# A two-layer cross-attention kernel: queries laid once over two halves of the partitions

## What is computed

```python
q_hk  = (hidden_q @ Wq.T).reshape(B, S, H, K)
q_big = einsum('bshk,hkq->bshq', q_hk, w_kc_q)        # 192 wide
q_big = apply_rope(q_big, sin_q, cos_q)               # layer 0 only
kv_r  = apply_rope(kv_c, sin_k, cos_k)                # 1500 x 64
q_r   = einsum('bshq,hqr->bhsr', q_big, W_qr)
k_r   = einsum('bld,hdr->bhlr', kv_r, W_kr)
attn  = softmax(einsum('bhsr,bhlr->bhsl', q_r, k_r))
ctx_c = einsum('bhsl,bld->bhsd', attn, kv_r)
out   = einsum('bhsd,hkd->bshk', ctx_c, w_kc_kv).reshape(B, S, H*K) @ Wo.T
```

## Time and profile before

| | |
|---|---|
| median of 3 runs | 3490.61 us (3485.57 to 3497.17) |
| profiled execution: its time | 3502.88 us |
| profiled execution: span | 3501.1 us |
| TensorE, matmuls | 3137.0 us busy, 90% |
| VectorE | 2264.2 us, 65% |
| GpSimd | 1689.7 us, 48% |
| ScalarE | 1349.1 us, 39% |
| mean granted TensorE clock | 0.938 of 2.4 GHz |

### The profile page before, as it was taken

The page is one execution under the profiler, slowest core; times in us unless marked ns, Lnnn a source line. Parts: engine busy times, 40 slices in busy tenths (PEclk is TensorE's granted clock), DMA queues, the critical chain, the costliest instruction groups (busy, mean ns, idle before and its releaser), DMA issues. The chain is left out here.

```text
span 3501.1 us, 38073 instructions
## 1 busy us (share of the span) xinstructions
PE 3137.0 (90%) x12936; PEld 1862.8 (53%) x12936; DVE 2264.2 (65%) x3034; ACT 1349.1 (39%) x1939; POOL 1689.7 (48%) x984
## 2 busy tenths in 40 slices
PE   7699978999789998899988699879998799779997
PEld 6455456555465554655547455455545455454545
DVE  3578756788567885578856467546755477555755
ACT  3235533354342553425434244333433344333442
POOL 0467624676236762367733266315642366215641
PEclk9899989999899999899999799989998899899998
DMA  7411013111131110221102211111110211111110
GB/s 258 132 39 54 32 52 96 53 40 45 36 99 48 54 49 28 81 74 42 50 35 59 93 54 40 50 54 58 53 50 6 77 53 42 47 57 55 54 53 6
DMA packets 95735, 206.20 MB, mean 59 GB/s; under 512 B 9967, under 2 KB 58783, under 8 KB 94134
## 3 DMA queue, kind: packets, MB, share of 16 engines
q1 hardware_dynamic: 95542, 203.61, 17.9%
HBM read 153.44 MB, written 49.91 MB: 58 GB/s over the span
## 5 line engine op out<-in xcount | busy, mean ns | idle before, releaser
L1211 POOL TENSOR_TENSOR sum_pool<-sum_pool,prob 125x896 f32<-125x896 f32 x472 | 996.6, 2111 | 232.9 <-ACT prob L1098 229.3
L1098 ACT ACTIVATE prob<-wide 125x896 f32<-125x896 f32 x768 | 704.8, 918 | 949.1 <-PE wide L866 945.1
L1324 DVE TENSOR_REDUCE maxpart<-single 128x1 f32<-128x500 f32 x1344 | 823.8, 668 | 282.6 <-PE single L841 282.1
L880 PE MATMUL single<-prob,kv 125*64 125x448 f32 x3072 | 752.1, 568 | 0.8
L863 PE MATMUL wide<-qhigh,kparts 128*125 128x448 f32 x1536 | 523.4, 422 | 10.2 <-DMA kones<-keys_merged 10.2
L863 PEld LDWEIGHTS wide<-qhigh,kparts 128*125 128x125 f32 x1536 | 231.3, 189 | 504.8 <-issue 503.4
L866 PE MATMUL wide<-qlow,kones 65*125 65x448 f32 x1536 | 445.6, 372 | 0.0
L841 PE MATMUL single<-kparts,qhigh 128*128 128x500 f32 x1344 | 406.4, 409 | 17.0 <-DVE kparts L1292 5.9
L1211 POOL TENSOR_TENSOR sum_pool<-prob 125x896 f32<-125x896 f32 x64 | 134.8, 2105 | 392.5 <-ACT prob L1098 392.5
L866 PEld LDWEIGHTS wide<-qlow,kones 65*125 65x125 f32 x1536 | 292.2, 190 | 29.8
L841 PEld LDWEIGHTS single<-kparts,qhigh 128*128 128x128 f32 x1344 | 257.5, 193 | 80.6 <-issue 26.1
(11 more groups left out here) (272 smaller groups left out, 4414.1 us busy)
## 6 DMA issues: line engine op xcount, KB each, us to landing
wexp_low_values<-in_experts SPq DMA_DIRECT2D x68, 384.0 KB, 3.1
keys_merged<-kparts SPq DMA_DIRECT2D x32, 750.0 KB, 4.8
kparts<-keys_merged SPq DMA_DIRECT2D x32, 750.0 KB, 4.6
raw<-in_ctx SPq DMA_DIRECT2D x33, 375.0 KB
w_low_values<-w_merged SPq DMA_DIRECT2D x64, 192.0 KB, 2.4
values_merged<-kv SPq DMA_DIRECT2D x32, 375.0 KB
kv<-values_merged SPq DMA_DIRECT2D x32, 375.0 KB
kones<-keys_merged SPq DMA_DIRECT2D x96, 125.0 KB, 2.6
```

The lines of the kernel that those rows point to most:

```text
L880: mm = pe.matmul(mix_acc[64 * half:64 * half + DC, 0:HQ], kv[:, j % 3, t, :], prob[:, (j * LT + t) % NPROB, half * HQ:(half + 1) * HQ], st ...
L1098: nc.scalar.activation(prob[:, n_ % NPROB, :].rearrange("p (a b) -> p a b", a=2), acc[0:LP, :, 0:HQ], ACT.Exp)\
L1211: nc.gpsimd.tensor_tensor(dst, first_in, prob[:, n_ % NPROB, :], ALU.add).then_inc(s["pool_sum"], 1)
L1324: V.tensor_reduce(maxpart[:, j % 2, t, b:b + 1], acc[:, 0:LB], AX.X, ALU.max).then_inc(*R.signal_drained(kind, *key))
```

## The change

- The queries of heads 0 to 7 lie in partitions 0 to 63 and those of heads 8 to 15 in 64 to 127, in `qhigh` and `qlow` alike, once each. `kparts` has the high and the low part of the keys one behind the other in the columns, and both of them in both halves of the partitions. A score is four times two products of 64 partitions, one for each half: key-high x query-high, key-low x query-high, key-high x query-low, and ones x `shift` (the maxima, now a buffer of their own). `kones` and its copies are gone.
- Maxima: 4 tiles of TQ = 112 queries for each half x 3 thirds = 12 pairs of products (112 x 500 each), key-high x query-high alone, one pair in each step, four steps ahead (`EARLY_MAX = 4`). A pair fills one new region, `pair`, of two banks; regions 4 and 5 are its banks. A reduction takes both banks at once. keyT, maxT and norm share region 3 alone.
- Queries: heads n and n + 8 are made together. In layer 0 each half's product writes its own 64 partitions; in layer 1 the merged weights hold both heads, and 8 products take the place of 16. The layer's weight slots are 8.
- Layer 0: rope of batch j + 2 moves from step 10 to step 3, its keyT to steps 5, 6 and 7, each followed by a copy of the third to the other half of the partitions. Layer 1: the fetch loads the keys twice, once for each half.
- Reciprocals: two DMAs pack the sums of a batch (2 x 448) into 112 x 8, VectorE takes the reciprocal of those, one DMA stores it to DRAM, two spread it over the partitions. The last batch of a group stays as it was.

Its core as a diff:

```diff
-        pe.matmul(acc[:, 0:LB], qhigh[:, j, t * 128:(t + 1) * 128], kparts[:, kdst(j), b * LB:(b + 1) * LB],
-                  start=True, stop=True).then_inc(*R.signal_filled(kind, *key))
+        for half in range(2):
+            mm = pe.matmul(acc[0:TQ, half, 0:LB], qhigh[rows_of(half), j, t * TQ:(t + 1) * TQ],
+                           kparts[rows_of(half), j % 3, 0, b * LB:(b + 1) * LB], start=True, stop=True)
+        mm.then_inc(*R.signal_filled(kind, *key))
...
-        for half in range(2):
-            q = slice(half * HQ, (half + 1) * HQ)
-            pe.matmul(acc[0:LP, half, 0:HQ], kparts[:, kdst(j), cols], qhigh[:, j, q], start=True, stop=False)
-        for half in range(2):
-            q = slice(half * HQ, (half + 1) * HQ)
-            mm = pe.matmul(acc[0:LP, half, 0:HQ], kones[:, cols], qlow[:, j, q], start=False, stop=True)
+        for i, (part, q) in enumerate(((0, qhigh), (1, qhigh), (0, qlow))):
+            for half in range(2):
+                pe.matmul(acc[0:LP, half, 0:HQ], kparts[rows_of(half), j % 3, part, cols], q[rows_of(half), j, :],
+                          start=(i == 0), stop=False)
+        if t == 0:
+            pe.wait_ge(s["shift_loaded"], 32 * (j + 1))
+        for half in range(2):
+            mm = pe.matmul(acc[0:LP, half, 0:HQ], c["ones_row"][rows_of(half), 0:LP], shift[rows_of(half), j % 2, :],
+                           start=False, stop=True)
...
-        V.tensor_reduce(maxpart[:, j % 2, t, b:b + 1], acc[:, 0:LB], AX.X, ALU.max)
+        V.tensor_reduce(maxpart[:, j % 2, t:NMAX:4, b], acc[0:TQ, :, 0:LB], AX.X, ALU.max)
...
+        meets = {PAIR: (PAIR, 4, 5), 4: (4, PAIR), 5: (5, PAIR)}
...
         for t in range(LT):
+            ahead = (j + 1, t + EARLY_MAX) if t + EARLY_MAX < LT else (j + 2, t + EARLY_MAX - LT)
...
             add("score", j, t, region=t % 2)
-            for _ in range(SMAX_PACE[t]):
...
+            if ahead[0] < BG:
+                maximum(*ahead)
             if last is not None:
                 add("mix", *last)
...
+            if layer == 0 and t in (5, 6, 7) and j + 2 < BG:
+                keys(j + 2, t - 5)
+            if t == 3 and j:
+                add("spread", j - 1)
...
-            if layer == 0 and t == 10 and j + 2 < BG:
+            if layer == 0 and t == 3 and j + 2 < BG:
                 add("rope", j + 2)
...
+                    if kind == "keyT":
+                        sp.wait_ge(*R.drained("keyT", j, b))
+                        sp.dma_start(kparts[DC:2 * DC, j % 3, :, cols].bitcast(F32), kparts[0:DC, j % 3, :, cols].bitcast(F32))
...
+                    if kind == "norm" and key[0] < BG - 1:
+                        sp.wait_ge(*R.drained("norm", j))
+                        for half in range(2):
+                            sp.dma_start(packed[half * ZP:(half + 1) * ZP, :], total[64 * half:64 * half + 1, :])
+                    if kind == "spread":
+                        sp.wait_ge(s["packed_recip"], j + 1)
+                        sp.dma_start(scratch["zrec"][j].rearrange("(p c) -> p c", c=ZC), packed_recip[:])
+                        sp.wait_ge(s["recip_stored"], 16 * (j + 1))
+                        for half in range(2):
+                            sp.dma_start(recip[64 * half:64 * half + 64, :],
+                                         scratch["zrec"][j:j + 1, half * HQ:(half + 1) * HQ].broadcast_to([64, HQ]))
```

More of the change, by code:

```diff
@@ L83, in schedule, with keys, maximum, last_maxima @@
     steps = []
-    spin = [0]
     def add(kind, *key, region=None):
         steps.append((kind, key, region))
[L89 to L93, removed]
-        for c in range(3):
[L95 to L100, removed]
+    def keys(j, c):
+        add("keyT", j, c, region=3)
+    def maximum(j, n):
+        add("smax", j, n % 4, n // 4, region=PAIR)
+    def last_maxima(j):
+        for c in range(3):
+            add("smax", j, 3, c, region=PAIR)
     if layer == 0:
@@ L105, in schedule @@
         add("fetch", 0)
-    for h in range(SPLIT_AHEAD):
-        add("wsplit", h)
+    for n in range(SPLIT_AHEAD):
+        add("wsplit", n)
     if layer == 0:
         add("rope", 0)
[L110 to L131, removed]
@@ L132, in schedule @@
-    maxima(0, range(done, NMAX))
+        for c in range(3):
+            keys(0, c)
+        for n in range(H + 2):
+            if n == H - 3:
+                add("rotate", 1)
+            if n == H:
+                add("rope", 1)
+            if n + SPLIT_AHEAD < H:
+                add("wsplit", n + SPLIT_AHEAD)
+            if n < H:
+                add("qwide", n, region=n % 2)
+            if n >= 3 and n % 2:
+                add("query", (n - 3) // 2, region=2)
+            if n >= 7 and n % 4 == 3 and n < H:
+                for c in range(3):
+                    add("smax", 0, n // 4 - 1, c, region=PAIR)
+    else:
+        for p in range(NPAIR):
+            if p < 2:
+                add("fetch", p + 1)
+            if p + SPLIT_AHEAD < NPAIR:
+                add("wsplit", p + SPLIT_AHEAD)
+            add("query", p, region=p % 3)
+            if p >= 3 and p % 2:
+                for c in range(3):
+                    add("smax", 0, p // 2 - 1, c, region=PAIR)
@@ L133, in schedule @@
+    last_maxima(0)
     add("maxneg", 0)
-    add("maxT", 0, region=turn())
     if layer == 0:
-        keys(1)
-    maxima(1, range(EARLY_MAX))
+        keys(1, 0)
+    add("maxT", 0, region=3)
+    if layer == 0:
+        keys(1, 1)
+        keys(1, 2)
+    for n in range(EARLY_MAX):
+        maximum(1, n)
     last = None
-    for c in range(3):
-        add("kone", 0, c)
     for j in range(BG):
-        ahead = [(row, c) for row in range(EARLY_MAX if j == 0 else 0, NMAX) for c in range(3)] if j + 1 < BG else []
@@ L621, in run_layer @@
     steps = schedule(layer)
-    R = Regions(steps, [sems[f"filled_{i}"] for i in range(6)], [sems[f"drained_{i}"] for i in range(6)])
+    R = Regions(steps, [sems[f"filled_{i}"] for i in range(7)], [sems[f"drained_{i}"] for i in range(7)])
     s = sems
@@ L670, in _ @@
         def _(dve):
[L671 removed]
+            nc.vector.memset(shift[:].bitcast(F32), 0.0)
+            nc.vector.memset(maxneg[:], 0.0)
             dve.wait_ge(first_pe, 1)
@@ L874, in _ @@
                         if t == 0 and not j:
-                            last = H - 1 if layer == 0 else max(h for h in range(H) if h % 3 == 2)
+                            last = NPAIR - 1 if layer == 0 else max(p for p in range(NPAIR) if p % 3 == 2)
                             pe.wait_ge(*R.drained("query", last))
```

253 lines of the change are left out of this document (131 added, 122 removed).

## The result

The change makes the kernel slower: 3858.3 us median (3852.4 to 3869.9) against 3488.1 (3482.3 to 3497.2), a ratio of 1.105 with a 95% interval of 1.103 to 1.108. I had forecast 3567, in a range that ended at 3650: the direction is right, the size is 370 us where I had 76. The profiled execution has a span of 3860.3 us.

A forecast was written before the change was run, and what follows sets the result against it. TensorE, busy 90% of the span, was taken as the bound. Layer 0 +23 and layer 1 -3.3 us a group, four of each, less 3 for setup, gave +76 us: median 3567 us, range 3430 to 3650.

The forecast's parts named there:

- the rope stall: Layer 0 loop, step 3: rope products wait for GpSimd's sums; TensorE stalls 4.3 us, six times a loop, 25.6 us.
- making of the queries: Before a group's loop: fewer query products, but maxima pairs in step with VectorE: +8 us layer 0, +3 layer 1.
- merging of the weights: Setup, last stage: products of 64 columns for 128, 3 us less, once.
- Maxima and score pairs: In the loop: a pair takes about one product's time; maxima save 14.0 us a loop, score 0, step 2.14 us.
- Rivals 2 and 3: Pairs somewhat slower than one product (3690 us, chance 0.12); pairs not running together (4225 us, chance 0.04).
- Rival 1: Rope at step 3: VectorE not blocked, 0.6 for 4.3 us, query stretches even: 3435 us, chance 0.27.
- Reduction: VectorE's reduction of a maxima pair: 1.19 us, 1.67 us from pair to pair, hidden below the 2.14 us step.
- Norm, 0.6 us: Start of a batch: TensorE waits 0.6 us for VectorE's last sums, batches 1 to 6: 3.4 us a loop.
- Reciprocals in layer 1: Layer 1 loop: packing copies behind the larger fetch land at 12.5, pair 5 0.9 us late: 4.3 us in 5 batches.
- Keys twice: Three copies of 250 KB behind keyT 5 to 7, needed at step 8: hidden, 0 to 1 us.

The follow-up runs named there:

- e2: Changed kernel with the small reciprocal and its copies at step 6 instead of step 3 in layer 1: 3726.4 us.
- e11: Changed kernel with GpSimd's sums in layer 0 cut to 8 columns from 896, from the third tile of a batch on, last batch excepted: 3730.3 us.
- e4: Changed kernel with layer 0's loop rope products moved to step 11 of the batch before and step 0, rotation to step 10: 3734.5 us.
- e5: Changed kernel with the keys stored in DRAM as 128 rows, 1500 KB a batch, and fetched as two transfers of 128 rows: 3796.5 us.
- e3: Changed kernel with layer 0's stores of values and keys issued after the shift copies (step 9) instead of before (step 7): 3772.9 us.
- e8: e6 with the maxima pairs of the making of the queries spread among the wide products or queries instead of three in a row: 3530.6 us.
- e10: e9 with rotation, rope and transposing of batch 1's keys among the wide products in layer 0's making of the queries: 3502.4 us.
- e12: e10 with the norm products at step 2 instead of 1, and layer 0's small reciprocal at step 4 instead of 3: 3499.1 us.
- e13: e12 with GpSimd's second rope product of the loop at step 2 instead of step 0: 3467.6 us, 0.992 of the kernel before.
- e6: Changed kernel with the changes of e2, e3 and e4 together: 3581.9 us.
- e9: e8 with the second rope product in layer 0's loop done by GpSimd at step 0 instead of VectorE: 3510.5 us.
- e1: Changed kernel with layer 1's keys fetched as two transfers of 128 rows x 6000 B instead of two of 64 rows x 12000 B: 4501.9 us.

## Why the prediction was right in direction and wrong in size

The direction came from the rope stall, which stands where I put it; it was no luck. But it holds for the whole only: for a group of layer 1 I had 3.3 us less, and it is 27.9 more. Four steps of the sum failed: the time at which the packing copies land in layer 1; the price of a wait of TensorE in the loop (its own length, without the clock); the shift copies, which the sum left out; and the clock in the making of the queries and in the merging of the weights. By place, for all four groups together, from the two traces (in layer 1 the making of the queries is taken from the last ctx_raw of the group before, with the feed-forward part):

| place | forecast | measured |
|---|---|---|
| layer 0, loops | +60 | +165 |
| layer 0, making of the queries | +32 | +74 |
| layer 1, loops | -25 | +76 |
| layer 1, making of the queries | +12 | +35 |
| merging of the weights | -3 | +10 |
| all | +76 | +359 |

(What is left out is -1 us between them. The medians of the runs differ by 370: the profiled execution of the kernel before was 12 us above its median.)

- **Maxima and score pairs.** Right. Two halves run together (step 2.14 us). With the waits of layer 1 gone (e2) batches 1 to 7 take 5 x 27.3 + 26.2 + 22.9 = 185.6 us against 6 x 28.9 + 22.9 = 196.3: 10.7 less, and with six norm waits of 0.48 us put back 13.6. Of the sum's 14.0 these batches hold 12.7 (126 products less 68 pairs). Rivals 2 and 3 fall. Rival 1 falls by the rope stall itself.
- **Reduction.** 1.20 us, forecast 1.19.
- **Rope, 4.3 us.** Right in place and mechanism: 3.67 measured, products of 2.55 and 2.72 us (forecast near 2.5 and 3). e11 shows the cause. But a stall costs more than its wait: e4 gives 124 us for 4 x 25.6 = 102. The step that failed is that I let the clock fall only in the making of the queries, and in the loop counted a wait at its own length.
- **Norm, 0.6 us.** In layer 1 0.5; in layer 0 hidden behind the stalls.
- **Reciprocals in layer 1, 4.3 us a loop (0 to 10).** This term failed most. I gave the added 750 KB 0.9 us; they were written to 64 rows at a time, where the rate is about half (e5), and the copies landed 15.5 us after score 0 (2764.3 to 2779.9) where I had 12.5. So the pair was 3.65 us late and not 0.9, the clock fell behind it, and a loop lost 5 x 6.6 = 33 us (e2), three times my upper bound. 4 x (33 - 4.3) = 115 us of the miss.
- **Shift copies.** Not in the sum. I asked what stands behind the moved keys' copies on SyncE, and not what stands behind the stores in the DMA queues, which now go out just ahead of the shift and take 8.6 us. 85 us (e3).
- **Making of the queries, +8 and +3.** +18 and +9 measured. In layer 0 e8 takes back 11 of the 18 by spreading the triples: the waits of 2.0 and 1.3 us and the clock that falls behind them, for which I had only a part of +1. In layer 1 e8 takes back 3; and TensorE waits 3.7 to 4.6 us for the first keys of each group, where before it waited 2.4 to 2.8 us for the kones; the sum did not have this. 4 x (10 + 6) = 65 us.
- **Merging of the weights, -3.** +10 measured. The last stage has as many products as before, of 64 columns in place of 128, and takes 25.3 us in place of 14.5. TensorE is busy in it without a gap, but from 81 us on the granted clock is 0.50; before it was 1.00 throughout (windows of the kernel before, first, and of the changed one, columns as in the earlier trace rows). 13 us of the miss. That the narrow products lowered the clock fits, and no run tests it.

```profile
76.00:91.00 15.00, 14.53 (x128) 14.37 (x128) 4.71 (x17) 4.44 (x16) 0.00 (x0) 1.00 0.01 1
```

```profile
96.00:103.00 7.00, 7.00 (x34) 6.98 (x33) 0.90 (x4) 0.89 (x4) 0.00 (x0) 0.50 0.00 0
```

- **Keys twice.** Hidden in layer 0: no wait of TensorE is put down to the second copies.

76 + 115 + 85 + 65 + 13 + 22 (rope) = 376 against 370 measured. The savings of e2, e3 and e4 overlap (276 of 341 us), so this is a reckoning of single effects, not a proof that nothing else is in it. What is left between the loops of layer 0 in e8 (8 us more than before) was not taken apart beyond e10.

## What to carry to other kernels

When a rotating set of buffers becomes one, every late operation of the engine that empties it stalls the one that fills it: list what that engine waits for (DMAs too) and what it shares with a third engine, and put those where the buffer isn't wanted. Cost a transfer by its rows as well as its bytes, and a small urgent copy by the large ones ahead of it in the queues. Look behind each wait of TensorE for slow time: here it cost 1.5 us (rope) and 2.9 us (reciprocal) on top of waits of 3.7 us, and nothing on top of the waits of 2.3 us in e12. Mended in this way the change is 0.8% faster than the kernel before (0.6 to 1.0%), not 10% slower. The mended kernel also has a rope product on GpSimd and a new order in the making of the queries; what these would give the kernel before was not tried.

## What the runs showed of the hardware

- In the loops of the changed kernel waits of TensorE of 3.2 to 4.3 us were followed by products at the lower clock (granted 0.50) until 2.4 to 6.3 us behind the wait, and waits of 1.7 to 2.2 us for the shift until 2.8 to 6.7 us behind. But 20 waits of 2.0 to 2.4 us in e12 had no slow product behind them (granted 1.00), and neither had those of 0.5 and 0.8 us in e13: the length of the wait alone did not decide it.
- The clock also fell without a wait: in the merging of the weights TensorE ran products of 64 columns without a gap, and from 81 to 103 us the granted clock was 0.50; with products of 128 columns, as many of them, it was 1.00 (76 to 91 us of the kernel before).
- Two operations with two inputs in SBUF, one on VectorE and one on GpSimd, took 2.60 and 3.14 us when they met, and 1.09 and 1.82 apart. The wait follows the collision wherever it is put (e6, e9, e12).
- In the store of the keys 750 KB landed in 8.6 us from 64 rows, and 1500 KB in 7.6 us from 128 rows (e5); the transfers of e1, whose source has an outermost size of 2, moved 52 GB/s.
